# Masked attention block: edge masks used untransposed as stationary operands, first stage re-ordered, key placement in larger transfers

## The reference

```
h  = relu(layernorm(x)); hs = layernorm(h)*g1+b1; ht = layernorm(h_target)*g1+b1      # sources, targets
q, k, v = ht@Wq+bq (over sqrt 32), hs@Wk+bk, hs@Wv+bv                                # 8 heads
logits  = where(adj != 0, q.k, -1e30); probs = softmax(logits); ctx = probs@v
ht = layernorm(ht + ctx@Wo + bo)*g2+b2
out = x + ht + gelu(ht@W1)@W2                                                        # W1 256x1024, W2 1024x256
```

## Time and the profile before

| | |
|---|---|
| three runs | 769.35 us median (768.35 to 772.59) |
| profiled execution | 769.7 us, span of its trace 767.7 us |
| PE busy, PEld busy | 684.5 us (89%), 432.9 us (56%) |
| DVE, ACT, POOL busy | 566.8, 488.9, 525.0 us |
| first stage, up to the first `scores` | 96.8 us |
| units 0 to 31, up to the last copy of the context | 96.8 to 666.8 us |
| tail | 666.8 to 767.7 us |

### The profile page before, as it was taken

One profiled execution on the slowest core, in us unless ns is written; L12 is line 12 of the kernel. 1 busy time (PEld: TensorE's weight loads), 2 busy tenths in 40 slices (PEclk: granted clock), 3 DMA queues, 4 the chain that ended last, 5 costly groups with the idle time before them and its releaser, 6 DMA issues.

```text
span 767.7 us, 17726 instructions
## 1 busy us (share of the span) xinstructions
PE 684.5 (89%) x6997; PEld 432.9 (56%) x7106; DVE 566.8 (74%) x969; ACT 488.9 (64%) x877; POOL 525.0 (68%) x505
## 2 busy tenths in 40 slices
PE   3684689999989899899998999999999898889998
PEld 2352545565555566565555665656556465447667
DVE  4623859887978878988888887987877896265651
ACT  3454557875668655767885576776556787676550
POOL 4430039986859887777997876789897899934430
PEclk9997989999999899999999999999999999999999
DMA  8165300110301000002110000130000003000001
GB/s 285 48 166 146 114 1 29 57 55 29 97 29 56 29 29 29 2 19 79 57 37 21 29 29 1 43 125 2 1 2 2 2 2 111 1 1 15 22 21 56
DMA packets 23858, 36.06 MB, mean 47 GB/s; under 512 B 2752, under 2 KB 19424, under 8 KB 23776
## 3 DMA queue, kind: packets, MB, share of 16 engines
q1 hardware_dynamic: 23776, 34.92, 14.8%
HBM read 26.49 MB, written 2.10 MB: 37 GB/s over the span
## 4 chain that ended last, share of the span: by engine, by line
PE 37%; POOL 8%; DVE 3%; ACT 2%; issue 2%; another core or an unknown queue 0%; DVEq 0%; ACTq 0%
PE score L420 15%; PE early L420 12%; PE ctx L420 6%; POOL prob_lo L1374 6%; PE aux L420 3%; DVE early L1172 1%; POOL mask_nat L1408 1%; ACT prob L873 1%; POOL mask_T L1414 1%; DVE prob_lo L1180 1%; PE aux L476 0%; ACT qT L1049 0%; DVE q_stage L1203 0%; ACT L873 0%
## 5 line engine op out<-in xcount | busy, mean ns | idle before, releaser
L1374 POOL TENSOR_TENSOR prob_lo<-prob 128x512 f16<-128x512 f32 x384 | 433.1, 1151 | 131.1 <-ACT prob L873 130.7
L873 ACT ACTIVATE prob<-score 128x512 f32<-128x512 f32 x512 | 304.9, 597 | 168.5 <-PE score L420 139.2
L420 PE MATMUL early<-kT,qT 96*128 96x512 f16 x512 | 194.9, 386 | 22.5 <-DMA kT<-mask_nat 9.8
L420 PE MATMUL score<-qT,kT 97*128 97x512 f16 x512 | 198.9, 388 | 10.7 <-ACT prob L873 9.2
L420 PE MATMUL ctx<-v_sb,prob 128*128 128x65 f16 x2048 | 194.1, 194 | 6.5 <-POOL prob_lo L1374 4.2
L420 PEld LDWEIGHTS ctx<-v_sb,prob 128*128 128x128 bf16 x2048 | 160.5, 98 | 68.3 <-ACT raw L895 12.7
L1172 DVE CUSTOM_DVE_ANT_0 early<-early,mask_nat,half_max 128x1024 f32<-128x1024 f32 x128 | 164.0, 1286 | 46.2 <-PE early L420 44.2
L420 PE MATMUL ctx<-v_sb,prob_lo 128*128 128x65 f16 x2048 | 192.9, 194 | 0.0
L1172 DVE CUSTOM_DVE_ANT_0 early<-early,mask_nat 128x1024 f32<-128x1024 f32 x128 | 156.9, 1230 | 42.4 <-PE early L420 36.0
L420 PEld LDWEIGHTS ctx<-v_sb,prob_lo 128*128 128x128 f16 x2048 | 144.9, 98 | 47.0 <-issue 6.2
L420 PE MATMUL score<-mask_T,nidentb 128*128 128x512 bf16 x403 | 156.0, 387 | 0.0
(11 more groups left out here) (165 smaller groups left out, 718.3 us busy)
## 6 DMA issues: line engine op xcount, KB each, us to landing
adj_in<-in_adj SPq DMA_DIRECT2D x28, 512.0 KB, 3.7
qT<-q_stage SPq DMA_DIRECT2D x48, 64.0 KB, 2.0
kT<-mask_nat SPq DMA_DIRECT2D x48, 64.0 KB, 2.1
raw<-in_x SPq DMA_DIRECT2D x4, 512.0 KB, 5.8
tgt<-in_L_gnn_h_target SPq DMA_DIRECT2D x4, 512.0 KB, 5.2
prob<-in_adj SPq DMA_DIRECT2D x4, 512.0 KB, 9.4
mask_nat<-in_L_gnn_W SPq DMA_DIRECT2D x2, 1024.0 KB, 6.3
mask_nat<-in_x SPq DMA_DIRECT2D x1, 2048.0 KB, 8.1
```

The lines of the kernel that those rows point to most:

```text
L420: return nc.tensor.matmul(dst, w, m, start=start, stop=stop, **more)
L873: nc.scalar.activation(prob[:, n % SLOTS, :], score[n % 2][:, :], ACT.Exp).then_inc(exp_done, 1)
L1374: nc.gpsimd.tensor_tensor(prob_lo[:, n % SLOTS, :], prob[:, n % SLOTS, :], prob_hi(n % SLOTS), ALU.subtract).then_inc(lo_sem["pool"], 1)
```

## The change

Scores take the mask from `mask_nat` directly: four matmuls, each with a 128x128 block of the mask as the stationary operand and the 128 columns of `nidentb` moving, open the accumulation, and the matmul of keys and queries closes it. `mask_T`, its transposes and its copies are gone. All eight first masks are made on DVE from eight buffers of their own; the later masks' ACT passes stand in r = 0 to 3 of the block before. `kT` is laid out by chunk, and heads are stored in an order in which one DMA reads and writes 1024 neighbouring values for each partition; the first three DMAs of a chunk have a semaphore of their own. The first stage's order, the places of the side jobs and the loads of W1, W2 and x are changed.

```diff
-SLOTS = 7
+SLOTS = 8
-MT_FIRST = {(4, 5): 0, (5, 1): 1, (5, 4): 2, (5, 11): 3, (5, 14): 4, (6, 1): 5, (6, 4): 6, (6, 11): 7}
-MT_LATER = {(0, 13): 0, (1, 11): 1, (1, 14): 2, (2, 5): 3, (5, 1): 4, (5, 4): 5, (5, 11): 6, (5, 14): 7}
-CT_AT = {(1, 1): 0, (1, 4): 1}
-WO_AT = {(2, 1): 0, (2, 11): 1}
-QT_AT = {(3, 1): 0, (3, 4): 1}
+CT_AT = {(2, 1): 0, (2, 4): 1}
+WO_AT = {(2, 11): 0, (3, 1): 1}
+QT_AT = {(3, 5): 0, (3, 11): 1}
-HT_AT = {(6, 1): 0, (6, 4): 1}
+HT_AT = {(7, 1): 0, (7, 4): 1}
-FREE = (2, 4, 7, 11, 13, 15)
-MASK_FIRST = [(0, s) for s in (7, 11, 13)] + [(r, s) for r in (1, 2) for s in FREE] + [(3, 7)]
-MASK_EARLY = [(r, s) for r in (6, 7) for s in FREE]
-MASK_LATE = [(0, s) for s in FREE[:4]]
+MASK_ACT = [(0, s) for s in (7, 11, 13)] + [(r, s) for r in (1, 2) for s in (2, 4, 7, 11, 13, 15)] + [(3, 7)]
+MASK_DVE = [(3, 1), (4, 1), (4, 5), (5, 2)]
+SUM_AT = [(0, 5), (0, 11), (1, 3), (1, 9)]
+NORM_AT = [(0, 4), (0, 7), (1, 3), (1, 6)]
+def head_of(r):
+    return r % 2 * TT + r // 2
+        def masks_free(eng, k):
+            if k == 1:
+                for c in range(NTB):
+                    eng.wait_ge(k_first[c], FIRST)
+                    eng.wait_ge(k_placed[c], PLACE - FIRST)
+            else:
+                eng.wait_ge(score_ready, (k - 1) * H * STEPS)
+                def place(dst, stage, g, part, r, done):
+                    sp.dma_start(dst[r * HD:(r + 1) * HD, 2 * g:2 * g + 2, :].rearrange("p h t -> p (h t)"),
+                                 stage[g * HD:(g + 1) * HD, part, :, :].rearrange("p m t -> p (m t)")).then_inc(done, 16)
...
                 place_q(0)
-                load_adj(0, 5)
                 for c in (1, 2):
                     sp.dma_start(tgt[:, c * TT:(c + 1) * TT, :], rows(h_target, c)).then_inc(tgt_in[c], 16)
                 place_k(0)
-                load_adj(0, 6)
-                place_k(1)
-                load_adj(0, 7)
-                place_k(2)
-                place_k(3)
+                for i in range(TT, PAIRS):
+                    load_adj(0, i)
+                for c in range(1, NTB):
+                    place_k(c)
...
-                    mm(score[n % 2][:, :], kT[0:ROWS + 1, h, m * P:(m + 1) * P], q_block(k)[0:ROWS + 1, h, :], True, False)
-                    mm(score[n % 2][:, :], nidentb[:, :], mask_T[:, k % 2, m, :], False, True).then_inc(score_ready, 1)
+                    for t in range(TT):
+                        mm(score[n % 2][:, t * P:(t + 1) * P], mask_nat[:, k % 2, t, m * P:(m + 1) * P], nidentb[:, :],
+                           t == 0, False, skip_group_check=True)
+                    last = mm(score[n % 2][:, :], kT[0:ROWS + 1, m // TT, h, m % TT * P:(m % TT + 1) * P],
+                              q_block(k)[0:ROWS + 1, h, :], False, True, skip_group_check=True)
+                    last.then_inc(score_ready, 1)
...
                 project(0)
-                for g in range(1, 4):
-                    turn_rows(g + 1)
-                    project(g)
-                    values(g - 1)
...
+                project(1)
+                turn_rows(2)
+                values(0)
+                turn_rows(3)
+                project(2)
+                values(1)
+                turn_rows(4)
+                project(3)
+                values(2)
                 project(4)
...
-                for e in range(done, RAMP):
+                for e in range(TT):
                     for i in range(2):
                         early_scores(e, i)
-                    turn_first_mask(e - 1)
-                turn_first_mask(PAIRS - 1)
+                    values(e + 3)
+                values(7)
+                for e in range(TT, RAMP):
+                    for i in range(2):
+                        early_scores(e, i)
...
-                for k in range(1, 3):
-                    target_deviation(k)
-                first_mask_out(PAIRS - 1)
                 negated(0)
...
-                        if k == 1 and o == 0:
-                            act.wait_ge(nT_masked, DC * NTB)
-                            for c in (2, 3):
-                                act.wait_ge(k_placed[c], PLACE)
-                        if k > 1 and o == 0:
-                            act.wait_ge(max_done, (k - 1) * H * PAIRS)
+                        if o == 0:
+                            masks_free(act, k)
...
-                            if r == 3 and s == 12:
+                            if r == 5 and s == 15:
                                 row_deviation(k - 1, lead_width(k - 1))
-                            if r == 5 and s in (2, 4, 7, 11):
+                            if r == 6 and s in (2, 4, 7, 11):
                                 second_norm(k - 1, (2, 4, 7, 11).index(s))
```

More of the change, by code:

```diff
@@ L317, in value_bank @@
         def value_bank(i):
-            return early[1][:, i % 2 * TB:(i % 2 + 1) * TB] if i < NT // 4 else (ctx, aux)[i % 2][:, :]
+            if i < 2:
+                return early[1][:, i * TB:(i + 1) * TB]
+            return (score if i < 4 else (ctx, aux))[i % 2][:, :]
         def raw_of(k):
@@ L974, in _ @@
                 high_values(1)
-                for o in range(4, 8):
-                    mask_op(0, o)
+                for k in range(1, 3):
+                    target_deviation(k)
+                nc.scalar.activation(warm_c, eps_c, ACT.Exp).then_inc(act_link, 1)
                 features(4)
@@ L998, in _ @@
                     k, r = divmod(u, H)
-                    masks = {s: (kk, o) for s, kk, o in mask_ops(u)}
+                    masks = {s: o for o, (rr, s) in enumerate(MASK_ACT) if rr == r and k + 1 < NTB}
                     for s in range(STEPS):
@@ L1140, in low_parts @@
                         bias = Q_B if what == "t0" else BK
-                        hi, lo = ((q_stage[:, i, m, :] if what == "t0" else k_stage[:, what % 2, i, m, :]) for i in range(2))
+                        hi, lo = ((q_stage[:, i, m, :] if what == "t0" else k_stage[:, what, i, m, :]) for i in range(2))
                         nc.vector.scalar_tensor_tensor(out=lo, in0=(ctx, aux)[m][:, :], scalar=bias[:, m:m + 1], in1=hi,
@@ L1239, in _ @@
                 target_stats(0)
+                target_norm(0)
                 second_stats(0)
[L1241 to L1242 removed]
                 second_scale(0)
@@ L1252, in _ @@
                                                op1=ALU.subtract).then_inc(q_b, 1)
+                second_stats(1)
+                second_scale(1)
+                first_stats(3)
                 second_stats(2)
-                first_stats(3)
+                low_parts(0)
                 second_scale(2)
                 second_stats(3)
-                low_parts(0)
+                low_parts(1)
                 second_scale(3)
-                low_parts(1)
+                for i in range(2):
+                    make_mask(0, i)
                 low_values(0)
+                for i in range(2, TT):
+                    make_mask(0, i)
+                for k in range(1, 3):
+                    target_stats(k)
                 low_parts(2)
                 low_values(1)
+                make_mask(0, 4)
                 low_parts(3)
                 low_values(2)
-                maxima(0)
+                make_mask(0, 5)
                 low_parts(4)
-                low_values(3)
-                for i in range(NT // 4, NT // 2):
-                    make_mask(0, i)
-                    maxima(i - NT // 4 + 1)
-                    low_values(i)
-                for e in range(NT // 4 + 1, RAMP):
-                    maxima(e)
-                for k in range(1, 3):
-                    target_stats(k)
+                for e in range(TT):
+                    maxima(e)
+                    low_values(e + 3)
+                    if e < 2:
+                        make_mask(0, e + 6)
+                low_values(7)
+                for e in range(TT, RAMP):
+                    maxima(e)
                 for u in range(UNITS):
```

262 lines of the change are left out of this document (97 added, 165 removed).

## The result

The changed kernel takes 742.42 us (median of 4 runs, 736.74 to 742.72); the kernel before, beside it, 770.13 (4 runs, 768.35 to 772.59). The ratio is 0.9621, with a 95% interval of 0.9566 to 0.9675: 3.8% faster. The direction was forecast, the size was not: 27.7 us instead of 47.2, and 742.4 is above the range's 740. The profiled execution took 742.36 us, its span is 740.6.

What follows compares the result with a forecast made beforehand. PE was taken to bound quiet units, SP's issue queue much of the first stage, POOL unit 25. 24 + 1.5 + 11 - 3 + 9.6 + 5.6 - 1 + 1 - 1.5 = 47.2 us off 769.7: 722 us, eight in ten 709 to 740.

Steps and rivals of the forecast that it cites:

- The step that failed: Side jobs of the main part: ACT's table change for `row_deviation` moves from r = 3 to r = 5, priced at nothing.
- the list of what would show me wrong: Signs: mask matmuls 80 ns or more apart, early scores waiting beyond 66 us, new PE waits in r = 1 to 3.
- The first stage: Start to first score: first score at 72 to 73 against 96.8, 24 us gained, bounds 19 and 28.
- the start: First stage, SP's chain: `place_q` starts at about 26.5, 10.4 us earlier.
- The rate: First stage, SP's issue: one placement taken as 0.6 us, bounds 0.40 and 0.70, the old ones 0.65 to 0.7.
- Rival (a): First stage gives back half, a waiting DVE instruction holding the rest: 10 to 14 us less gained, 732 to 736; chance 0.18.
- Table load and clock: Behind the first score: table load done early, PE perhaps starting above half clock; 1.5 us gained, bounds 0 and 3.
- Transposes and mask matmuls: Masks in the steps: 24 transpose jobs removed, 11 us gained; four mask matmuls per step at 56 ns, 3 us lost.
- Waits that go: PE's waits for context transposes in units 9 and 17, 9.6 us; ACT's for a maximum in units 6 and 14, 5.6.
- POOL: Two `context_sum` fewer in units 8 and 16, +1 us; two more in unit 25, which POOL bounds, -1.5.
- the -1 for units 12 and 20: Units 12 and 20: two DVE mask passes beside the query products cost 1 us.
- my forecast in blocks 1 and 2: Main part, forecast terms put beside each block: 11.0 us gained in block 1, 6.2 in block 2.

Runs made afterwards that it cites:

- run 1: The changed kernel with ACT's four `second_norm` operations later in r = 6 (steps 7, 11, 13, 15), the chain otherwise unmoved; 730.59 us.
- run 2: The changed kernel with the whole chain `lead_stats`, `row_deviation`, `lead_scale`, `second_norm` moved back to r = 3 to 5; 728.38 us.
- Run 10: The changed kernel with chain early (late in block 3), late mask and target loads early, first masks behind chunk 1's low parts, block 3's sums in unit 24; 721.89 us.
- run 7: The changed kernel with the four mask matmuls of each step issued twice; 828.62 us (one run).
- Run 4: The kernel before with only the masks changed (four mask matmuls, no transposes, new mask places); first stage and other side jobs as before; 759.37 us.
- run 8: The changed kernel with block 3's four `context_sum` all in unit 24, none in unit 25; 737.55 us.
- run 6: The changed kernel with DVE's first masks made behind the low parts of chunk 1 instead of in front of them; 741.36 us.
- run 9: The changed kernel with the second norm's chain early (r = 3 to 5) in blocks 1 and 2, late (r = 3 to 6) in block 3; 728.24 us.

## Why the prediction was wrong

**The step that failed** is the sentence "ACT's table change for `row_deviation` goes from r = 3 to r = 5: nothing". I priced the two table loads, which are the same wherever they stand, and not the chain that moves with them: DVE's four statistics into unit 13, beside the mask pass of (5, 2), where DVE had 0.4 us to spare, and `second_norm` to the step in which DVE comes to `lead_scale`, where 20 steps had lain between. The second price could be had from the rows that I showed. ACT's instruction waits at the head of a queue of exponentials, the very pattern of the earlier trace rows, which I counted as a gain where it goes. Runs 1 and 2 show it: 11.8 us come back when ACT merely asks later, 14.0 when the chain is back early, of which about 11 are the chain's. Of the 8.8 and 6.5 us that blocks 1 and 2 were short, run 2 gives back 6.0 and 4.5. In block 3, 2.3 short, the late chain lengthens units 29 (15.2 to 17.7, POOL busy throughout in both) and 30 (16.1 to 17.8); run 1 takes the wait out of unit 30. In the list of what would show me wrong I named waits in r = 1 to 3 only.

**The first stage** is 3 us short of 24, within its bounds. It is short by more against its own terms: the last maximum at 69.5 and 1.7 us behind it give a first score at 71.2, not 72 to 73. Measured, the maximum ends at 74.04. The term was the start: placements at 27.84, not 26.5, and the second chunk of keys at 47.68, where my sum (26.5 + 24 x 0.65 + 3.4) has 45.5. The rate was right. Two things held the second chunk that I hadn't in my streams, POOL's doubled pass and the wait for the target load. Run 10 has both away and gains 25.7, at a third projection in full clock. Rival (a) named the right kind of thing in the wrong place: a waiting DVE instruction ahead of the low parts, with a load issued too late behind placements; but it was the target load ahead of `low_parts(2)`, not `make_mask` ahead of `low_parts(3)`, and it cost a fraction of 10.

**Table load and clock**, 1.5 us: nothing. Unit 0 takes 28.75 us instead of 28.53. PE starts at half clock in both (0.50 and 0.52 in the first 4.2 us) and keeps it longer now (0.80 in the next 4 us instead of 1.00).

**Transposes and mask matmuls**, +11 and -3: right as far as they can be told apart. The step grew by 0.01 us, and run 7 prices a mask pair at 55 to 58 ns. The Trainium skill's 81 ns for a sustained stream of such pairs ("TensorE: Matmul & The Clock Gate", section "Back-to-back issue gap") isn't borne out by these rows.

**Waits that go**, +9.6 and +5.6: they went. Unit 9 is at 15.84 and 17 at 15.83, forecast 15 to 16; unit 6 at 14.90. Units 14 and 22 would be (run 2: 14.90), had the chain not put a new wait there. Run 4 shows that it takes the moved sums, norms and context transposes to free unit 17 (no run tells the three apart), and that the masks' new places, with the transposes gone, free 6 and 14. Of the 6.3 for unit 9 about 3 were the half clock of that one trace, which unit 17 didn't have.

**POOL**, -1.5 in unit 25: it was -1.9, and run 8 shows the sums as the cause. The +1 for units 8 and 16 didn't come (15.6 and 15.7 before, 15.7 now), nor did the -1 for units 12 and 20 (18.3 and 19.3 before, 18.3 now). Unit 24, with equal streams, was 21.6 in the changed kernel and 20.0 in run 1, at a granted clock of 0.84 and 0.91: not a matter of the change.

**What stays open.** Run 2 is still 2.8 and 2.0 us above my forecast in blocks 1 and 2 (133.2 and 133.9). Its units 11 and 12 are at 19.9 and 19.3, above the 17.9 and 18.3 of before, with PE busy for 18 us and more; I didn't take these two apart.

## What to carry to other kernels

When a side job moves, price every instruction of its chain at the new place, and above all the distance between the one that makes a value and the one that asks for it: an instruction that waits in front of ACT's exponentials costs PE the wait and, as often in these traces, a stretch at half clock behind it. Cut before and after at the same unit ends and put each term of the sum beside its stretch; here blocks 1 to 3 pointed at the step that failed. Two small causes on parallel paths of a first stage can hide behind each other: 0.1 and 0.2 us alone, 3.6 together, of which some 2 may be the clock's. Compare a trace with one that had the same clock there.

## What the runs showed of the hardware

- POOL's four passes of 128x256 took 4.08 us while DVE turned int32 into bfloat16 masks, 2.16 us without that (run 6 shows it by moving the masks alone; run 9, with the masks beside a pass that starts at the same time, has 4.10).
- A DMA of 32 partitions took 591 ns to issue with one run for each partition and 597 ns with two.
- The clock after an idle stretch isn't a function of this stretch alone: behind 2.9 us of idle time the next four matmuls of a projection took 1.96 us in run 10 and 3.75 in run 6. With equal streams unit 24 was 20.0 or 21.6 us long, unit 14 19.4 or 20.9, and the first stage of run 9, which is that of the changed kernel, ended 1.1 us earlier. A few us between two traces with no edit in between are to be expected, and are no effect.
